# A two-layer graph network on one core: first layer with POOL left to gather, one-input run masks, digits in thirds, re-placed picks and a deferred normalisation

## The chip, the cores and the metric

The kernel runs on 1 core of one Trainium2 chip. The metric is device time in microseconds (us); the median of 3 runs of the kernel before is 3593.15 us (3582.03 to 3596.72).

## The reference

6250 nodes have 128 features, 200,000 edges (sorted by `dst`) have a source, a destination and one of 8 types, and every node has one of 4 types. Two residual layers follow each other:

```
# first layer (x + relu(concat(x, neighbour mean) @ W.T + b), then layer norm)
neigh_sum = segment_sum(x[src], dst)
mean = neigh_sum / max(deg, 1)
neigh_agg = where(deg > 0, mean, x)
x = layernorm(x + relu(concat([x, neigh_agg]) @ W.T + b))
# second layer: typed attention over the edges of each dst
Q, K, V = typed_matmul(x, W_Q | W_K | W_V, node_type)
scores = sum(Q[dst] * typed_matmul(K[src], W_edge, edge_type)) / sqrt(128) * mu[edge_type]
attn = segment_softmax(scores, dst)
x = layernorm(x + segment_sum(V[src] * attn, dst))
```

## The kernel before

Nodes are cut into 49 tiles of 128, edges into columns of 128. The columns are taken in periods of 32; the first layer walks over 49 such periods, one a step (`sweep(l0)`, i = 0 to 48, ND = TILES = 49). Of a period's 32 columns, 14 are fetched by POOL with indirect DMAs ("gathered", two runs of HALF = 7 columns), and 18 (GCOLS) are done on the chip ("dense"), by one-hot masks.

The five instruction streams are written out by hand, and semaphores join them. In each one, the text gives the order in which it executes.

- **POOL**: after setup it issues 98 groups of 7 gathers, group k into buffer k mod 3 (`near`, RUNS = 3), and from the fourth group on it waits before each until TensorE has summed the run that last used the buffer (`runs_ps`). Before the third group it computes `edge_keys()` (src*8 + edge type for every edge, three instructions of 1664 columns), and before the fourth `weights()` (8 small ones on the edge weights).
- **PE** (TensorE), `l0`: 49 matmuls `slot_sum(i, h)`, h = 0 to 48, each of 385 columns, carry the step. Between them stand 18 `pick(i+1, c)` at the h of PICK_AT (they build the next step's one-hot `picked`), the two `run_sum` of 7 matmuls at h = 2 and 23 (RUN_AT), `node_sum` at 6, and the projections of two node tiles: `early` = i-2 (transposes of x and of the mean, the first product) and `late` = i-3 (transpose of the normalised tile at 9, key and value projections at 16 and 18, `low_keys` at 27, `high_keys` at 30).
- **ACT** (ScalarE), `l0`: `take(i+1, c)` copies pick c out of PSUM bank c mod 2, so pick c + 2 waits for it. Between the takes stand `copy_key`, `copy_projected`, `copy_high`, `copy_x`, `copy_mean` and `deviation` (a square root).
- **DVE** (VectorE), `l0`: `hot` builds the masks of 3 picks at a time in a ring of 9 (HOT_RING); `belong(i, h)` builds the 7 masks of a run; `join_parts`, `add_nodes` and `add_runs` add up; `mean`, `relu`, `normalise_x1` belong to the early tile, `by_types` and `copy_low` to the late one. In steps 4 to 12, one `digit_op` (9 in all, 1664 columns each) prepares the second layer's masks.
- **SP** issues the plain DMAs of each tile: the normalised rows and their typed copy to DRAM, the loads of x and of the types two tiles ahead, and the tile's 1 MB of `kv_table` (`store_table`). `store_digits()` is six DMAs, ahead of tile 12.

After the first layer come 98 blocks of the second, each of 16 indirect gathers on POOL (L722) and its attention. The change doesn't touch their code.

Of the kernel before, what the change touches and what calls it, by code (L numbers as in the profile page):

```python
# [6 lines left out]
ALU = mybir.AluOpType  # L7
# [7 lines left out]
P = 128  # L15
# [23 lines left out]
def gnn_kernel(nc, x, src, dst, etype, ntype, w0, b0, wq, wk, wv, we, mu, out):  # L39
# [53 lines left out]
    with ExitStack() as ctx:  # L93
# [47 lines left out]
        iota_g = sb("iota_g", [P, P])  # L141
# [37 lines left out]
        spare_f = spare_n[:, :].bitcast(F32)  # L179
        spare_b = spare_n[:, :].bitcast(BF16)[:, 0:NAT]  # L180
# [28 lines left out]
        near_runs = [near_flat[:, 0:HALF * TW // 2], near_flat[:, HALF * TW // 2:], src_n[:, 0:HALF * TW // 2].bitcast(F32)]  # L209
# [219 lines left out]
        DIGIT_OPS = 9  # L429
        DIGIT_STEP = 4  # L430

# [52 lines left out]
        def _(sp):  # L484
# [85 lines left out]
            for t in range(TILES):  # L570
                if t == 12:
                    sp.wait_ge(digit_vec, DIGIT_OPS)
                    store_digits()
                store(tile(t))
                if t < TILES - 1:
                    store_table(tile(t))
                else:
                    store_last_table(t)
# [73 lines left out]
        def _(pool):  # L652
# [37 lines left out]
            def weights():  # L690
                pool.wait_ge(L["small"], 16)
                pool.wait_ge(L["weights"], 80)
                for e in range(ET):
                    pool.tensor_scalar(we_s[:, e, :], we_s[:, e, :], mu_b[:, e:e + 1], SCALE, ALU.mult, ALU.mult
                                       ).then_inc(weights_ready, 1)

            def edge_keys():
                pool.wait_ge(L["etype"], 48)
                pool.tensor_scalar(spare_n[:, :], src_n[:, :], float(ET), None, ALU.mult).then_inc(pool_step, 1)
                pool.wait_ge(pool_step, 2)  # L700
                pool.tensor_tensor(et_n[:, :], spare_n[:, :], et_n[:, :], ALU.add).then_inc(pool_step, 1)
                pool.wait_ge(pool_step, 3)
                pool.tensor_copy(key_f, et_n[:, :]).then_inc(keys_nat, 1)

            pool.wait_ge(parts_stored, 16 * (TILES // 7))
            pool.wait_ge(tab_copied, TABLES)
            for k in range(2 * ND):
                if k == RUNS - 1:
                    edge_keys()
                    pool.wait_ge(keys_nat, 1)  # L710
                if k == RUNS:
                    weights()
# [29 lines left out]
        def _(pe):  # L742
# [124 lines left out]
            PICK_AT = [-(-c * TILES // GCOLS) for c in range(GCOLS)]  # L867
# [3 lines left out]
            def l0(i, late, early):  # L871
                for h in range(TILES):
# [50 lines left out]
                    if i + 2 < ND and h == TILES - 1:  # L923
                        wait_hot(i + 2, 0)
# [44 lines left out]
            pe.wait_ge(keys_nat, 1)  # L969
# [132 lines left out]
        def _(act):  # L1102
# [64 lines left out]
            def l0(i, late, early):  # L1167
                for c in range(GCOLS):
# [8 lines left out]
                    if late and c == 11:  # L1177
                        copy_high(late)
                    if early and c == 11:
                        copy_x(early)  # L1180
                    if early and c == 13:
                        copy_mean(early)
                    if early and c == 16:
# [79 lines left out]
        def _(dve):  # L1263
# [216 lines left out]
            def digit_op(k):  # L1480

                dve.wait_ge(*((digit_vec, k) if k else (keys_nat, 1)))
                X, Y, Z = (digits[:, i, :] for i in range(3))
                if k == 0:
                    ins = dve.tensor_scalar(spare_n[:, :], dst_n[:, :], 3, 15, ALU.arith_shift_right, ALU.bitwise_and)
                elif k == 1:
                    ins = dve.tensor_scalar(X, spare_n[:, :], -2.0, 16.0, ALU.mult, ALU.add)
                elif k == 2:
                    ins = dve.tensor_scalar(spare_n[:, :], dst_n[:, :], 7, None, ALU.bitwise_and)
# [265 lines left out]
```

## Time and profile before

| | |
|---|---|
| median of the runs | 3593.15 us |
| the profiled execution | 3594.51 us |
| its span, first to last instruction | 3592.7 us |
| mean granted TensorE clock | 0.839 |
| busy PE, DVE, ACT, POOL | 2618.7, 1554.8, 1151.8, 2244.9 us |
| steps of the first layer | 72.6 to 1246.8 us |
| second layer | 1348.0 us to the end |

Busy time counts the engine's own instructions, not its waits; "PEclk" is the share of full speed that TensorE was granted. A row of a timeline has the start, the duration, the engine, line, operation and tiles, and in brackets the idle time before it with what ended it; "issue" and "remote" name no instruction of another engine. TensorE's rows begin when its queue takes an instruction up, and their ends are modelled.

### The profile page before, as it was taken

Reading aid. Unit: us, or ns where it says so; the run is one execution under the profiler, and the core shown is the slowest. Engines: PE = TensorE matmul, PEld = TensorE weight load, DVE = VectorE, ACT = ScalarE, POOL = GpSimd, SP = SyncE. Lnnn points to the kernel's source line nnn. Section 1 sums busy time; section 2 is a strip of 40 time slices with the busy share of each in tenths; the row PEclk is TensorE's granted clock in tenths of the full one; section 3 lists DMA queues with packets and bytes.
Section 4 is the critical chain, followed back from the end, with each engine's and each line's share of the span. In section 5 each row is a group of like instructions: output and inputs, shape, how many; then the busy total and the mean of one; then the engine's idle time right before and its main releaser. Section 6 shows DMA issues by size and latency. Waiting matters only on the chain.

```text
span 3592.7 us, 38408 instructions
## 1 busy us (share of the span) xinstructions
PE 2618.7 (73%) x13802; PEld 1868.6 (52%) x13802; DVE 1554.8 (43%) x4730; ACT 1151.8 (32%) x2057; POOL 2244.9 (62%) x2302
## 2 busy tenths in 40 slices
PE   3587888887878827777777777777777777777777
PEld 1355566555556625555554555555555555555555
DVE  8476677666667613322322233322322333323223
ACT  4344454444444412222222222222222222222222
POOL 7665566566556454666666666666666666666664
PEclk9799999899999968777778887777777877777778
DMA  6244354444444432333333333333333333333332
GB/s 157 62 129 121 111 144 130 120 126 120 119 119 126 118 122 75 100 99 100 100 100 101 103 100 100 99 97 100 100 100 102 102 100 101 100 99 100 101 100 69
DMA packets 256960, 384.03 MB, mean 107 GB/s; under 512 B 100640, under 2 KB 189003, under 8 KB 250625
## 3 DMA queue, kind: packets, MB, share of 16 engines
q0 software_dynamic: 108112, 273.13, 27.6%
q1 hardware_dynamic: 146833, 107.53, 9.7%
q8 instruction: 108, 1.77, 0.2%
q10 hardware_dynamic: 1824, 0.92, 0.1%
q14 instruction: 83, 0.68, 0.1%
HBM read 304.30 MB, written 77.13 MB: 106 GB/s over the span
## 4 chain that ended last, share of the span: by engine, by line
POOL 36%; PE 25%; issue 18%; another core or an unknown queue 13%; DVE 5%; ACT 2%; DMA 0%; ACTq 0%; DVEq 0%; POOLq 0%
POOL ring L722 35%; PE banks L777 9%; PE banks L769 4%; PE banks L803 3%; PE banks L850 1%; PE banks L862 1%; PE banks L992 1%; PE banks L855 1%; PE banks L1005 1%; ACT picks L1138 1%; PE banks L1029 1%; PE banks L865 1%; PE banks L1021 1%; POOL ring L717 1%
## 5 line engine op out<-in xcount | busy, mean ns | idle before, releaser
L722 POOL DMA_INDIRECT ring<-kv_table,src_n x1563 | 1485.4, 950 | 798.3 <-issue 447.6
L1005 PE MATMUL banks<-identf,ring 128*128 128x128 f32 x1568 | 436.9, 373 | 630.4 <-issue 501.1
L717 POOL DMA_INDIRECT ring<-x_part_rows,work x462 | 475.1, 1028 | 307.4 <-PE banks L803 142.8
L1005 PEld LDWEIGHTS banks<-identf,ring 128*128 128x128 f32 x1568 | 250.9, 182 | 791.1 <-issue 585.2
L777 PE MATMUL banks<-sums,picks 128*126 128x385 bf16 x2401 | 608.1, 342 | 33.3 <-ACT picks L1138 15.3
L1138 ACT ACTIVATE picks<-banks 128x343 bf16<-128x343 f32 x882 | 433.3, 512 | 543.7 <-PE banks L769 333.6
L1227 ACT ACTIVATE work<-banks 128x512 f32<-128x512 f32 x392 | 213.5, 598 | 887.6 <-remote 638.9
L1623 DVE SCALAR_TENSOR_TENSOR sums<-sums,corr,banks 128x128 f32<-128x128 f32 x98 | 34.0, 347 | 1029.2 <-remote 1022.6
L1219 ACT ACTIVATE work<-banks,negmax 128x2048 f32<-128x2048 f32 x98 | 192.8, 1968 | 807.9 <-issue 743.7
L777 PEld LDWEIGHTS banks<-sums,picks 128*126 128x126 bf16 x2401 | 331.6, 143 | 149.4 <-issue 54.1
L769 PE MATMUL banks<-sums 128*128 128x343 bf16 x882 | 286.1, 325 | 168.7 <-issue 105.8
L1604 DVE TENSOR_REDUCE largest<-banks 128x1 f32<-128x2048 f32 x98 | 224.5, 2291 | 370.5 <-PE banks L992 273.6
L1029 PE MATMUL banks<-ring,sums 128*128 128x128 f32 x3136 | 372.7, 277 | 5.6 <-issue 4.5
L992 PE MATMUL banks<-work,queries 128*128 128x512 f32 x784 | 372.8, 619 | 0.0
L1029 PEld LDWEIGHTS banks<-ring,sums 128*128 128x128 f32 x3136 | 358.6, 192 | 6.5 <-issue 5.1
L1661 DVE COPY sums<-banks 128x512 f32<-128x512 f32 x392 | 262.5, 689 | 148.6 <-PE banks L1021 101.7
L717 POOL DMA_INDIRECT src_n<-x_part_rows,work x224 | 232.5, 1038 | 136.6 <-issue 60.5
L1021 PE MATMUL banks<-identf,work 128*128 128x128 f32 x1568 | 313.0, 384 | 1.1 <-ACT work L1219 1.1
L1021 PEld LDWEIGHTS banks<-identf,work 128*128 128x128 f32 x1568 | 303.0, 212 | 2.4 <-ACT work L1219 1.3
L1383 DVE TENSOR_SCALAR sums<-iota_k,keys_g 128x344 bf16<-128x344 bf16 x882 | 288.4, 327 | 0.0
L1382 DVE TENSOR_SCALAR sums<-iota_n,keys_g 128x128 bf16<-128x128 bf16 x882 | 238.7, 271 | 114.3 <-PE banks L769 58.9
L992 PEld LDWEIGHTS banks<-work,queries 128*128 128x128 f32 x784 | 144.7, 195 | 189.7 <-issue 189.7
(260 smaller groups left out, 2363.3 us busy)
## 6 DMA issues: line engine op xcount, KB each, us to landing
kv_table<-ring SPq DMA_DIRECT2D x48, 1024.0 KB
ring<-kv_table,src_n POOLq DMA_INDIRECT x1563
sums<-x_typed SPq DMA_DIRECT2D x99, 128.0 KB
x_typed<-work SPq DMA_DIRECT2D x49, 256.0 KB
ring<-x_part_rows,work POOLq DMA_INDIRECT x462
x_part_rows<-sums SPq DMA_DIRECT2D x7, 675.5 KB, 7.1
src_n<-x_part_rows,work POOLq DMA_INDIRECT x224
sums<-x_rows SPq DMA_DIRECT2D x51, 64.0 KB
```

Source lines behind the costliest of these rows:

```text
L717: pool.indirect_dma_start(near[k % RUNS][:, j, :], None, part_dram, bass.IndirectOffsetOnAxis(ap=col_ids[:, first + j:first + j + 1], axis ...
L722: pool.indirect_dma_start(kv_ring[u][:, j, :], None, table, bass.IndirectOffsetOnAxis(ap=of, axis=0)).then_inc(l1_rows[2 * u + j // RUN], 16)
L769: pe.matmul(bank[c % 2][:, 0:KEYS], hot_low[:, c % HOT_RING, :], hot_key[:, c % HOT_RING, 0:KEYS], start=True, stop=True).then_inc(pick_ps, 1)
L777: mm = pe.matmul(bank[2 + i % 2][0:SLOTS, 0:3 * D + 1], picked[:, i % 2, h, 0:SLOTS], x_parts[:, h, 0:3 * D + 1], start=(h == 0), stop=(h ...
L992: mm = pe.matmul(bank[g], queries[:, :], keysT[:, g, :], start=False, stop=True, skip_group_check=True)
L1005: tr = pe.transpose(bank[KEY_BANK[g]][:, j * P:(j + 1) * P], kv_ring[k.u][:, g * 4 + j, 0:D], identf[:, :])
L1021: tr = pe.transpose(bank[PROB_BANK[g]][:, j * P:(j + 1) * P], probT[:, at:at + P], identf[:, :])
L1029: mm = pe.matmul(bank[7][:, 0:D], prob[:, j, :], kv_ring[k.u][:, j, D:2 * D], start=(j == 0), stop=(j == COLS - 1))
L1138: act.activation(picked[:, par, :, c * NW:(c + 1) * NW], bank[c % 2][:, 0:KEYS].rearrange("p (h w) -> p h w", w=NW), ACT.Copy).then_inc(pi ...
L1382: dve.tensor_scalar(hot_low[:, c % HOT_RING, :], iota_n[:, :], keys_g[:, par, 1, c:c + 1], None, ALU.is_equal)
L1383: ins = dve.tensor_scalar(hot_key[:, c % HOT_RING, :], iota_k[:, :], keys_g[:, par, 0, c:c + 1], None, ALU.is_equal)
L1661: dve.tensor_copy(prob[:, g * 4:(g + 1) * 4, :].rearrange("p a b -> p (a b)"), bank[PROB_BANK[g]]).then_inc(prob_copied, 1)
```

## The change

In the first layer alone:

- `edge_keys` and `weights` leave POOL. DVE computes the weights in step 0, and the keys in steps 1 and 2, in four pieces of 416 columns with one fused instruction each. POOL's 98 groups stand back to back. The third run buffer moves from `src_n` to `spare_n`.
- `belong` becomes 7 one-input instructions with a column scalar, on a bf16 `iota_g`, in place of one two-input instruction over 896 elements.
- A `digit_op` covers a third of the columns: 27 of them in steps 4 to 30, after the step's hot masks and no longer at its head. `store_digits` moves from tile 12 to tile 30.
- PICK_AT is no longer even (0, 3, 6, 9, 11, ... 47) but a list. The HOT_AT waits follow from it. The wait for the first masks of the next step moves from h = 48 to h = 2.
- `normalise_x1` moves from the end of DVE's step i to step i+1, behind `join_parts`. ACT's `copy_high`, `copy_x`, `copy_mean` and `deviation` each stand one or two takes later.

```diff
-        near_runs = [near_flat[:, 0:HALF * TW // 2], near_flat[:, HALF * TW // 2:], src_n[:, 0:HALF * TW // 2].bitcast(F32)]
+        near_runs = [near_flat[:, 0:HALF * TW // 2], near_flat[:, HALF * TW // 2:], spare_n[:, 0:HALF * TW // 2].bitcast(F32)]
...
+        DIGIT_COLS = [k * CBLKS // 3 * P for k in range(4)]
+        DIGIT_ALL = 3 * DIGIT_OPS
         DIGIT_STEP = 4
+        KEY_OPS = 4
+        KEY_COLS = [k * NAT // KEY_OPS for k in range(KEY_OPS + 1)]
...
-                if t == 12:
-                    sp.wait_ge(digit_vec, DIGIT_OPS)
+                if t == 30:
+                    sp.wait_ge(digit_vec, DIGIT_ALL)
                     store_digits()
...
             for k in range(2 * ND):
-                if k == RUNS - 1:
-                    edge_keys()
-                    pool.wait_ge(keys_nat, 1)
-                if k == RUNS:
-                    weights()
                 if k >= RUNS:
...
-            PICK_AT = [-(-c * TILES // GCOLS) for c in range(GCOLS)]
+            PICK_AT = [3, 4, 7, 10, 14, 17, 18, 19, 22, 24, 25, 28, 29, 31, 33, 37, 42, 44]
...
-                    if i + 2 < ND and h == TILES - 1:
-                        wait_hot(i + 2, 0)
+                    if 0 < i < ND - 1 and h == 2:
+                        wait_hot(i + 1, 0)
...
-                    if late and c == 11:
+                    if late and c == 12:
                         copy_high(late)
-                    if early and c == 11:
+                    if early and c == 13:
                         copy_x(early)
-                    if early and c == 13:
+                    if early and c == 14:
                         copy_mean(early)
-                    if early and c == 16:
+                    if early and c == GCOLS - 1:
                         deviation(early)
...
-                dve.tensor_tensor(belongs[h], col_keys[:, 1, first:first + HALF].unsqueeze(2).broadcast_to([P, HALF, P]),
-                                  iota_g[:, :].unsqueeze(1).broadcast_to([P, HALF, P]), ALU.is_equal).then_inc(belongs_ready, 1)
+                for j in range(HALF):
+                    ins = dve.tensor_scalar(belongs[h][:, j, :], iota_g[:, :], col_keys[:, 1, first + j:first + j + 1], None,
+                                            ALU.is_equal)
+                ins.then_inc(belongs_ready, 1)
...
+            def weights():
+                dve.wait_ge(L["small"], 16)
+                dve.wait_ge(L["weights"], 80)
+                for e in range(ET):
+                    dve.tensor_scalar(we_s[:, e, :], we_s[:, e, :], mu_b[:, e:e + 1], SCALE, ALU.mult, ALU.mult
+                                      ).then_inc(weights_ready, 1)
+
+            def edge_keys(k):
+                at = slice(KEY_COLS[k], KEY_COLS[k + 1])
                 if k == 0:
...
+                    dve.wait_ge(L["etype"], 48)
+                dve.scalar_tensor_tensor(key_f[:, at], src_n[:, at], float(ET), et_n[:, at], ALU.mult, ALU.add
+                                         ).then_inc(keys_nat, 1)
...
+            def digit_op(n):
+
+                dve.wait_ge(*((digit_vec, n) if n else (keys_nat, KEY_OPS)))
+                part, k = divmod(n, DIGIT_OPS)
+                at = slice(DIGIT_COLS[part], DIGIT_COLS[part + 1])
...
             def l0(i, late, early):
-                if DIGIT_STEP <= i < DIGIT_STEP + DIGIT_OPS:
-                    digit_op(i - DIGIT_STEP)
                 if i > 0:
                     join_parts(i - 1, (i - 1) % 2)
+                if late:
+                    normalise_x1(late)
...
+                if i == 0:
+                    weights()
+                if 1 <= i <= KEY_OPS // 2:
+                    for k in range(2 * i - 2, 2 * i):
+                        edge_keys(k)
+                if DIGIT_STEP <= i < DIGIT_STEP + DIGIT_ALL:
+                    digit_op(i - DIGIT_STEP)
                 if late:
                     copy_low(late)
...
-                if early:
-                    normalise_x1(early)
```

## Rows read from the trace of the kernel before

**Rows 1.** Busy time by stage: us, then PE, PEld, DVE, ACT, POOL, clock, DMA share, GB/s.

```profile
143.50:461.80 318.30, 255.73 (x1437) 176.83 (x1436) 219.78 (x846) 142.62 (x311) 185.48 (x182) 0.94 0.42 116
461.80:1246.80 785.00, 657.21 (x3790) 465.56 (x3790) 546.07 (x2160) 365.46 (x797) 472.84 (x455) 0.94 0.43 124
1348.00:3592.70 2244.70, 1618.79 (x8205) 1169.25 (x8204) 676.06 (x1427) 570.42 (x830) 1439.80 (x1515) 0.79 0.34 98
```

**Rows 2.** The same view, seven steps of 21 us: the first and the sum.

```profile
481.13:502.19 21.06, 18.50 (x113) 13.24 (x113) 16.53 (x67) 10.80 (x25) 14.67 (x15) 1.00 0.48 138
...
sum 147.98, PE 128.65 PEld 92.57 DVE 115.69 ACT 75.87 POOL 102.98; mean PE 18.38 PEld 13.22 DVE 16.53 ACT 10.84 POOL 14.71
```

**Rows 3.** The same view, six steps of 19 us and eight of 30 us: their sums.

```profile
sum 117.10, PE 109.56 PEld 79.65 DVE 96.75 ACT 66.56 POOL 77.28; mean PE 18.26 PEld 13.27 DVE 16.13 ACT 11.09 POOL 12.88
...
sum 236.85, PE 173.06 PEld 117.44 DVE 136.50 ACT 87.56 POOL 129.13; mean PE 21.63 PEld 14.68 DVE 17.06 ACT 10.95 POOL 16.14
```

**Rows 4.** Timeline of POOL behind a step of 30 us, then in one of 21 us.

```profile
1127.33 1.96 POOL L717 DMA_INDIRECT src_n<-x_part_rows,work  x1 [9.78 <-PE banks L803]
...
1148.94 1.68 POOL L717 DMA_INDIRECT ring<-x_part_rows,work  x1 [1.26 <-remote]
1150.93 0.95 POOL L717 DMA_INDIRECT ring<-x_part_rows,work  x1 [0.30 <-issue]
...
1159.62 0.95 POOL L717 DMA_INDIRECT src_n<-x_part_rows,work  x1 [1.43 <-remote]
...
1162.13 1.50 POOL L717 DMA_INDIRECT src_n<-x_part_rows,work  x1 [0.30 <-issue]
...
1170.08 1.68 POOL L717 DMA_INDIRECT ring<-x_part_rows,work  x1 [1.39 <-remote]
```

**Rows 5.** Timeline of DVE in the same step of 21 us: run masks and hot masks.

```profile
1148.71 1.09 DVE L1414 TENSOR_TENSOR ring<-work,iota_g 128x896 bf16<-128x896 f32 x1 [0.58 <-remote]
...
1161.71 1.09 DVE L1414 TENSOR_TENSOR more_belongs<-work,iota_g 128x896 bf16<-128x896 f32 x1
...
1165.69 0.22 DVE L1382 TENSOR_SCALAR sums<-iota_n,keys_g 128x128 bf16<-128x128 bf16 x1
1165.83 0.42 DVE L1383 TENSOR_SCALAR sums<-iota_k,keys_g 128x344 bf16<-128x344 bf16 x1
```

**Rows 6.** Timeline of POOL at the start: the keys, the weights, and groups 3 and 4.

```profile
77.53 4.44 POOL L699 TENSOR_SCALAR spare_n<-src_n 128x1664 int32<-128x1664 int32 x1
...
87.73 1.05 POOL L717 DMA_INDIRECT src_n<-x_part_rows,work  x1 [0.28 <-POOL et_n L703]
...
97.06 3.64 POOL L694 TENSOR_SCALAR ring<-ring,mu_b 128x128 f32<-128x128 f32 x8
100.97 1.01 POOL L717 DMA_INDIRECT ring<-x_part_rows,work  x1 [0.27 <-issue]
```

**Rows 7.** Timeline of PE in step 1 (95.3 to 143.5 us): the two run sums.

```profile
98.71 2.43 PE L803 MATMUL banks<-src_n,ring 128*128 128x385 bf16 x7 [2.87 <-DMA src_n<-x_part_rows,work]
111.33 0.34 PE L803 MATMUL banks<-ring,more_belongs 128*128 128x385 bf16 x1 [4.94 <-DMA ring<-x_part_rows,work]
```

**Rows 8.** Waits of PE from 58.6 to 143.5 us: us in total, times, longest us.

```profile
PE banks L769 <- issue: 18.6, 5, 7.4
```

**Rows 9.** Waits of PE from 461.8 to 1246.8 us, the same columns.

```profile
PE banks L769 <- issue: 68.8, 61, 2.2
...
PE banks L769 <- ACT picks L1138: 26.6, 13, 4.2
```

**Rows 10.** Busy time by stage, steps 4 to 12.

```profile
190.82:409.49 218.67, 177.94 (x1008) 123.20 (x1008) 156.59 (x595) 98.43 (x217) 129.46 (x128) 0.95 0.43 121
```

**Rows 11.** Groups of DVE: busy us, mean ns, then idle time before them.

```profile
L1493 DVE SCALAR_TENSOR_TENSOR digits<-digits 128x1664 bf16<-128x1664 bf16 x1 | 1.9, 1883 | 0.0
...
L1337 DVE SCALAR_TENSOR_TENSOR picks<-picks,ring 128x1664 f32<-128x1664 int32 x1 | 3.5, 3521 | 0.0
...
L1478 DVE COPY ring<-banks 128x512 f32<-128x512 f32 x34 | 23.5, 692 | 83.6 <-remote 60.8 <-PE banks L862 22.0 <-issue 0.8
```

More of the change, by code:

```diff
@@ L140, in gnn_kernel @@
         run_sums = sb("run_sums", [P, D + 1])
-        iota_g = sb("iota_g", [P, P])
+        iota_g = sb("iota_g", [P, P], BF16)
         pick_cols = sb("pick_cols", [P, 3])
@@ L178, in gnn_kernel @@
         key_idx = src_n[:, :].bitcast(U32)
-        spare_f = spare_n[:, :].bitcast(F32)
-        spare_b = spare_n[:, :].bitcast(BF16)[:, 0:NAT]
+        half_b = src_n[:, :].bitcast(BF16)[:, 0:NAT]
         def parts(tile, at, end):
@@ L689, in _ @@
                                         ).then_inc(gen_loaded, 16)
[L690 to L703, printed above, removed]
             pool.wait_ge(parts_stored, 16 * (TILES // 7))
@@ L967, in _ @@
             late_part(tile(TILES - 1))
-            pe.wait_ge(keys_nat, 1)
+            pe.wait_ge(keys_nat, KEY_OPS)
             pe.wait_ge(picked_ready, ND * GCOLS + 2)
@@ L1478, in copy_low @@
                 dve.tensor_copy(kv_of(tile)[:, 0:4, 0:D], by_type(bank[6])).then_inc(kw_low, 1)
-            def digit_op(k):
-                dve.wait_ge(*((digit_vec, k) if k else (keys_nat, 1)))
-                X, Y, Z = (digits[:, i, :] for i in range(3))
-                if k == 0:
-                    ins = dve.tensor_scalar(spare_n[:, :], dst_n[:, :], 3, 15, ALU.arith_shift_right, ALU.bitwise_and)
+            def weights():
[6 more added lines that the diff above has]
+                at = slice(KEY_COLS[k], KEY_COLS[k + 1])
+                if k == 0:
+                    dve.wait_ge(L["etype"], 48)
[5 more added lines that the diff above has]
+                at = slice(DIGIT_COLS[part], DIGIT_COLS[part + 1])
+                X, Y, Z = (digits[:, i, at] for i in range(3))
+                near_dst, spare_d = dst_n[:, at], src_n[:, at]
+                half = half_b[:, at]
+                if k == 0:
+                    ins = dve.tensor_scalar(spare_d, near_dst, 3, 15, ALU.arith_shift_right, ALU.bitwise_and)
                 elif k == 1:
-                    ins = dve.tensor_scalar(X, spare_n[:, :], -2.0, 16.0, ALU.mult, ALU.add)
+                    ins = dve.tensor_scalar(X, spare_d, -2.0, 16.0, ALU.mult, ALU.add)
                 elif k == 2:
-                    ins = dve.tensor_scalar(spare_n[:, :], dst_n[:, :], 7, None, ALU.bitwise_and)
+                    ins = dve.tensor_scalar(spare_d, near_dst, 7, None, ALU.bitwise_and)
                 elif k == 3:
-                    ins = dve.tensor_scalar(Y, spare_n[:, :], -2.0, 8.0, ALU.mult, ALU.add)
+                    ins = dve.tensor_scalar(Y, spare_d, -2.0, 8.0, ALU.mult, ALU.add)
                 elif k == 4:
@@ L1494, in digit_op @@
                 elif k == 5:
-                    ins = dve.scalar_tensor_tensor(spare_b, Y, 0.25, Y, ALU.mult, ALU.mult)
+                    ins = dve.scalar_tensor_tensor(half, Y, 0.25, Y, ALU.mult, ALU.mult)
                 elif k == 7:
-                    ins = dve.tensor_scalar(spare_b, dst_n[:, :], 0.0, FAR_PLACE, ALU.is_lt, ALU.mult)
+                    ins = dve.tensor_scalar(half, near_dst, 0.0, FAR_PLACE, ALU.is_lt, ALU.mult)
                 else:
-                    ins = dve.tensor_tensor(Z, Z, spare_b, ALU.add)
+                    ins = dve.tensor_tensor(Z, Z, half, ALU.add)
                 ins.then_inc(digit_vec, 1)
             def l0(i, late, early):
-                if DIGIT_STEP <= i < DIGIT_STEP + DIGIT_OPS:
-                    digit_op(i - DIGIT_STEP)
                 if i > 0:
                     join_parts(i - 1, (i - 1) % 2)
+                if late:
+                    normalise_x1(late)
                 if i + 1 < ND:
@@ L1558, in _ @@
             join_parts(ND - 1, (ND - 1) % 2)
+            normalise_x1(tile(TILES - 3))
             before, last = tile(TILES - 2), tile(TILES - 1)
```

## The prediction, made before the change was run

> **What bounds the kernel now.** I read the busy time by stage first. The second layer takes 2244.7 of the 3592.7 us, and its code stays; the change works in the first layer, 1103.3 us from step 2 to its end [rows 1]. The later 34 steps take 785.0 us, 23.1 us each, with TensorE busy 657.2 us of them and the granted clock at 0.94 [rows 1]. So TensorE is the fullest engine, but on the mean it stands for 3.8 us of a step, and the question is what for.
>
> The same view step by step shows that a mean step hardly exists. Three kinds stand out among the 33 full later steps: seven of 21.1 us (147.98 / 7) [rows 2], six of 19.5 us (117.10 / 6) and eight of 29.6 us (236.85 / 8) [rows 3]; the other twelve lie between these. TensorE's work is nearly the same in the first two kinds, 18.4 and 18.3 us, so 19.5 us is about what the chain of matmuls needs, and what lies above it is waiting. In the long kind TensorE shows 21.6 us because its clock has dropped, and POOL waits 9.8 us for a run sum behind one [rows 4].
>
> The timeline of POOL says what sets the 21 us kind. A group of 7 gathers starts at 1148.94, the next at 1159.62 and the third at 1170.08: 10.7 and 10.5 us, together one step. Before each start POOL waited only 1.26 to 1.43 us [rows 4]. I read this as a ring of one length: a run sum is seen as done, POOL starts a group, and the next run sum is not seen as done before that group's time has passed. The reader is to see that a group then costs its own length plus some 1.4 us, and that anything that stretches a gather stretches the step. Two gathers of a step are stretched: the usual one is 0.95 us, but those at 1148.94 and 1162.13 take 1.68 and 1.50 [rows 4]. Just then DVE runs its two-input run masks, from 1148.71 and from 1161.71, 1.09 us each [rows 5].
>
> **The change part by part.** The sum is made against the profiled execution, 3594.5 us (span 3592.7, with 1.8 around it); the median of the runs is 1.4 lower.
>
> *Keys and weights leave POOL.* POOL spends from 77.53 to 87.73 us on the keys, 10.2 us, and 3.9 us from 97.06 to 100.97 on the weights [rows 6]. Behind them TensorE waits for the landing of its third and fourth groups, 2.87 and 4.94 us [rows 7]. Both groups now start 10 and 14 us earlier, and both waits go: 8 us. The same stage has 18.6 us of waits ahead of picks, up to 7.4 us each [rows 8]; they fall while POOL gathers without a pause, which it still will. I leave them, and take 0 and 26 us as the ends. On DVE the work comes back as four fused instructions, a quarter of one that takes 3.5 us [rows 11], so 0.9 us each, and eight small weight instructions, by a hot mask of more columns at most 0.4 us each [rows 5], 3 us in step 0. They stand ahead of `copy_low` and `add_runs`. In these steps DVE waits there for a run sum; if that cover is gone, they cost 3 us + 3.5 us.
>
> *Run masks with one input.* They are 14 small instructions a step for two of 1.09 us. The nearest row is the hot mask of the same shape and types: the next instruction starts 0.14 us behind it, and it lasts 0.22 [rows 5]. Seven are 1.0 to 1.5 us, so DVE gains and loses nothing to speak of. POOL gains 0.73 + 0.55 = 1.28 us a step if gathers beside small masks stay at 0.95. They do so now: 18 pairs of hot masks a step run beside the gathers, and the gathers at 1150.93 and 1159.62 take 0.95 [rows 4, 5]. That gain reaches the step only where POOL's ring sets it. Over 45 steps the ends are 0 and 58 us; I take half, 29 us, since the 19.5 us kind and the catching-up steps have other limits.
>
> The Trainium skill (SBUF — State Buffer, Who interferes with whom) says that a vector instruction with two SBUF inputs contends with GpSimd's reads; the rows of the mask agree, 1.68 for 0.95 us. It says too that a one-input copy or tensor_scalar in a two-port mode takes the same port pair for its whole length, which speaks against this change; by that, seven small masks would hold POOL about as long as one large one, and the sum would lose its 29 us. The hot masks' rows don't show it.
>
> *Digits in thirds.* Nine digit instructions of 1.0 to 1.9 us stand at the head of steps 4 to 12 [rows 11], ahead of `join_parts`, on which `node_sum` and the next masks hang. These nine steps take 218.67 us [rows 10], 24.3 each, 1.2 more than the later mean: 11 us in all. I take half, 5 us; the ends are 0 and 11. The 27 thirds cost some 0.4 to 0.6 us each and stand ahead of `copy_low`, where DVE waits 83.6 us over 34 steps, 2.5 a step [rows 11]. Without this cover they would cost up to 14 us. SP's six digit DMAs wait for tile 30 now; the order of the others stays.
>
> *Normalisation a step later.* DVE no longer waits for ACT's square root at its end, and `join_parts` goes ahead of it. The normalised tile is ready about 1 us later, but it is wanted only at h = 9, behind a run sum of 7 matmuls and nine slot sums. SP's store of the tile and the load of x two tiles ahead start later by the same 1 us, and that load is wanted a step later. Nothing, either way; what is late next would be `by_types`, with TensorE's projection at h = 16 behind it.
>
> *Picks and ACT's order.* TensorE's 68.8 us of idle before picks with no named releaser, and the 26.6 us that ACT's take ended [rows 9], are where placement can act. Picks 12 to 17 move up (h = 29 to 44 for 33 to 47), so the ring of masks frees earlier and DVE can run ahead; picks 5, 6 and 7 now stand at 17, 18 and 19, where the two projections lie between them. If those crowd ACT, each waits for a take. From the row I bound both sides at 27 us, and take a third as gain, 9 us.
>
> *Long steps.* Each costs 29.6 - 21.1 = 8.5 us more, eight of them 68 us. They show waits of TensorE and ACT on each other in the second half of the step, and POOL idle behind. The moved picks and the shorter groups both change the phases that lead there; no row says how far. The ends are 68 us gained and 68 lost (twice as many). I take half of them gone, 34 us, since more slack in POOL's ring and earlier masks both pull that way.
>
> Sum: 8 + 29 + 5 + 9 + 34 = 85 us, 3594.5 - 85 = 3509.5, and 1.4 less as a median: **3508 us**. Its own range is 3460 to 3560.
>
> **The rivals.** *All steps in the ring.* Every step takes 21.1 - 1.3 = 19.9 us. The stage from step 2 on is 47 steps in 318.3 + 785.0 us [rows 1], against 47 x 19.9 = 935; with the 8 us of the start the gain is 176 us: 3417. For it speaks that the 19.5 us steps exist [rows 3]; against it, that phases drift again as soon as one wait is missed.
>
> *The small masks hold POOL.* The gathers beside them stay at 1.5 us or more, no 29 us, and the phases stay, no 34: 3594.5 - 22 = 3572. Against it stand the hot masks' rows [rows 4, 5].
>
> *Only the start and the digits count.* Elsewhere TensorE's chain and its hand-overs with ACT set the step, and faster gathers only wait longer: 3594.5 - 8 - 5 = 3581. For it speaks TensorE's 18.4 of 21.1 us.
>
> *More long steps, slower.* Picks at 17, 18, 19 make takes and the key copy queue on ACT, TensorE stands once more in a step, POOL idles 9.8 us as it does behind a long step [rows 4]. At 8.5 us each, five more eat the 42 us of start, masks and digits; eight more give 3594.5 - 42 + 68 = 3620. Against it stands that ACT is busy only 10.8 of 21 us [rows 2].
>
> **How the numbers follow.** Changes under 0.5% (18 us) can't be told from none here: faster is below 3575, slower above 3611. Chances: my forecast 0.45; all in the ring 0.16; masks hold POOL 0.11, of which 0.07 below 3575; start only 0.15; more long steps 0.13. Faster 0.45 + 0.16 + 0.07 = 0.68; same 0.04 + 0.15 = 0.19; slower 0.13. The range takes in the three middle cases and half of the ring case: 3425 to 3605, which leaves out about 0.08 below and 0.12 above.
>
> **What would show it.** Right: step 1 without waits for gathers and well under 48 us; every gather at 0.95 us; seven small masks in 1.0 to 1.5 us; steps 4 to 12 no longer than the later ones; steps of 20 us and at most four of 29; DVE still idle before `copy_low`. Wrong: gathers of 1.5 us beside the masks; TensorE waiting for takes at picks 5 to 7; DVE no longer idle before `copy_low`; as many long steps as before, or more. What would make the number wrong is above all the count of long steps.

## The result and the profile after

The changed kernel takes 3683.89 us (median of 4 runs, 3670.47 to 3685.33) against 3589.63 (4 runs, 3582.03 to 3596.72): ratio 1.0264, interval 1.0224 to 1.0304, 2.6% slower. Predicted were 3508 us, 3425 to 3605.

The profiled execution of after took 3670.5 us. Its page begins (compare the table of the kernel before):

```profile
span 3668.7 us, 39015 instructions
...
PE 2658.7 (72%) x13802; PEld 1881.4 (51%) x13802; DVE 1561.7 (43%) x5348; ACT 1140.3 (31%) x2057; POOL 2206.0 (60%) x2291
```

Busy time of the first layer of after by stage (steps 0 to 2; 3 to 12; 13 to 47). The last line of the first block, and the second block, are the same 29 steps, 18 to 46, in after and in before. Columns: us, PE, PEld, DVE, ACT, POOL, granted clock, DMA share, GB/s.

```profile
78.78:148.78 70.00, 50.07 (x259) 31.98 (x258) 43.36 (x200) 26.33 (x57) 45.85 (x47) 0.89 0.27 67
148.78:407.43 258.65, 203.48 (x1120) 139.45 (x1120) 167.25 (x774) 108.75 (x241) 136.14 (x140) 0.93 0.40 113
407.43:1311.62 904.19, 713.82 (x3921) 485.04 (x3922) 586.01 (x2708) 376.35 (x840) 470.13 (x483) 0.93 0.40 113
...
534.87:1288.72 753.85, 594.44 (x3249) 403.27 (x3249) 486.17 (x2247) 311.79 (x696) 395.34 (x406) 0.93 0.40 114
```

```profile
523.34:1208.83 685.49, 566.94 (x3248) 399.89 (x3248) 475.20 (x1886) 319.64 (x697) 421.39 (x407) 0.93 0.43 123
```

All of the loss is in steps 3 to 47. Steps 0 to 2 take 70.0 us, where before took from 72.64 to 169.54, 96.9 us. But step 48 starts at 1311.62 us for 1231.42, 80.2 us later. The second layer, from its first to its last gather, takes 2281 us for 2283. The three kinds of steps are gone [rows 2, 3]: of the 29 steps none is under 24.2 or over 28.4 us, and the mean is 753.85 / 29 = 26.0 us for 23.6. Of these 2.35 us, (594.44 - 566.94) / 29 = 0.95 are TensorE's busy time and the other 1.4 its idle time.

Two groups of TensorE in the steps of after (485 to 1311 us) show where it stands: slot sums (L760) and picks (L752).

```profile
L760 PE MATMUL banks<-sums,picks 128*126 128x385 bf16 x1556 | 410.0, 340 | 85.2 <-ACT picks L1121 71.9 <-issue 7.3 <-DVE ring L1388 6.0
L752 PE MATMUL banks<-sums 128*128 128x343 bf16 x573 | 185.8, 324 | 89.6 <-issue 51.7 <-ACT picks L1121 37.9
```

Before, from 461.8 to 1246.8 us, the picks had 95.4 us of waits [rows 9], and the slot sums 17.5:

```profile
L777 PE MATMUL banks<-sums,picks 128*126 128x385 bf16 x1666 | 419.7, 341 | 17.5 <-issue 9.4 <-ACT picks L1138 7.9
```

Now the first slot sum of a step waits for the last take of the step before, 71.9 us in all, 2.3 a step. TensorE's timeline in step 31 of after, at h = 13 to 21 and at the start of the next step:

```profile
875.46 0.38 PE L760 MATMUL banks<-sums,picks 128*126 128x385 bf16 x1 [0.93 <-issue]
...
876.25 1.16 PE L833 MATMUL banks<-work,ring 128*128 128x128 f32 x8
...
877.41 0.31 PE L752 MATMUL banks<-sums 128*128 128x343 bf16 x1
...
877.87 1.05 PE L838 MATMUL banks<-ring,work 128*128 128x128 f32 x8
...
880.86 0.32 PE L752 MATMUL banks<-sums 128*128 128x343 bf16 x1 [1.78 <-issue]
...
895.91 0.90 PE L760 MATMUL banks<-sums,picks 128*126 128x385 bf16 x2 [2.35 <-ACT picks L1121]
```

TensorE stands still three times (I call this a stand): 0.93 us at h = 13, where it waits for `add_nodes`; 1.78 at the pick of h = 19, which needs ACT's take of the pick of h = 17; 2.35 at the next step's first slot sum. Behind the two long ones the clock falls (from 881.69 and from 895.69 us; the number behind the five engines is the clock), most of the time to its lower level, 1.2 GHz:

```profile
881.69:885.69 4.00, 3.53 (x12) 1.96 (x13) 1.24 (x6) 2.00 (x4) 0.30 (x1) 0.57 0.00 0
885.69:892.69 7.00, 7.00 (x40) 4.82 (x38) 5.18 (x21) 4.18 (x10) 5.47 (x6) 1.00 0.53 175
895.69:899.19 3.50, 3.28 (x11) 1.73 (x12) 3.33 (x17) 0.46 (x2) 0.00 (x0) 0.54 0.00 0
```

Added up over steps 18 to 46, the stands at the first slot sum are 66.9 us and those at the pick of h = 19 57.8, in all 29 steps; the one at h = 13 is 12.4 us, in 14 of them. The long ones wait for results that come late: in step 31 the first product was recorded to 892.26 us and the pick of h = 44 from 892.42, and ACT and DVE got on with them at 895.36 and 895.31.

```profile
895.31 0.29 DVE L1436 TENSOR_TENSOR ring<-banks,bias_b 128x128 f32<-128x128 f32 x1 [2.52 <-remote]
...
895.36 0.50 ACT L1121 ACTIVATE picks<-banks 128x343 bf16<-128x343 f32 x1 [0.35 <-remote]
```

POOL got what was promised and idles it away. Its gathers of the 29 steps take 974 ns (`ring<-`, x273), but it waits 174.6 us for run sums in that group and 76.9 in the other, 8.7 us a step. And DVE's seven small masks take 1.32 us, as forecast; the next instruction, `add_nodes`, starts 1.13 us behind their start:

```profile
873.87 1.32 DVE L1398 TENSOR_SCALAR ring<-iota_g,work 128x128 bf16<-128x128 bf16 x7
875.00 0.41 DVE L1388 TENSOR_TENSOR ring<-ring,banks 128x258 f32<-128x258 f32 x1
```

### The profile page after: what moved, and what is told of

It reads as the page before. It is cut to its first block, busy times and chain, and to the rows that moved or that the text cites. A ratio compares the mean times of both kernels' runs of the same rounds, so it can differ in the third digit from the quotient of the medians.

```text
span 3668.7 us, 39015 instructions
## 1 busy us (share of the span) xinstructions
PE 2658.7 (72%) x13802; PEld 1881.4 (51%) x13802; DVE 1561.7 (43%) x5348; ACT 1140.3 (31%) x2057; POOL 2206.0 (60%) x2291
## 4 chain that ended last, share of the span: by engine, by line
POOL 38%; PE 23%; issue 17%; another core or an unknown queue 14%; DVE 5%; ACT 3%; DMA 0%; DVEq 0%; ACTq 0%; POOLq 0%
POOL ring L705 38%; PE banks L760 8%; PE banks L752 5%; PE banks L786 4%; ACT picks L1121 2%; PE banks L845 1%; PE banks L833 1%; PE banks L838 1%; PE banks L848 1%; PE banks L775 1%; DVE sums L1366 0%; DVE sums L1365 0%; PE banks L975 0%; ACT work L1202 0%
## 5 line engine op out<-in xcount | busy, mean ns | idle before, releaser
L988 PE MATMUL banks<-identf,ring 128*128 128x128 f32 x1568 | 410.4, 366 | 618.4 <-issue 384.1
L760 PE MATMUL banks<-sums,picks 128*126 128x385 bf16 x2401 | 627.9, 341 | 123.3 <-ACT picks L1121 101.6
L700 POOL DMA_INDIRECT ring<-x_part_rows,work x462 | 449.5, 973 | 398.2 <-PE banks L786 264.0
L760 PEld LDWEIGHTS banks<-sums,picks 128*126 128x126 bf16 x2401 | 339.2, 144 | 257.2 <-ACT picks L1121 117.0
L752 PE MATMUL banks<-sums 128*128 128x343 bf16 x882 | 288.1, 327 | 142.8 <-issue 84.0
L975 PE MATMUL banks<-work,queries 128*128 128x512 f32 x784 | 391.6, 646 | 0.0
L700 POOL DMA_INDIRECT spare_n<-x_part_rows,work x224 | 218.1, 974 | 178.6 <-PE banks L786 115.1
L1004 PE MATMUL banks<-identf,work 128*128 128x128 f32 x1568 | 322.8, 392 | 1.1 <-ACT work L1202 1.1
L1004 PEld LDWEIGHTS banks<-identf,work 128*128 128x128 f32 x1568 | 311.3, 216 | 2.4 <-ACT work L1202 1.3
L1365 DVE TENSOR_SCALAR sums<-iota_n,keys_g 128x128 bf16<-128x128 bf16 x882 | 225.0, 255 | 165.2 <-remote 84.6
```

Source lines behind the costliest of these rows:

```text
L700: pool.indirect_dma_start(near[k % RUNS][:, j, :], None, part_dram, bass.IndirectOffsetOnAxis(ap=col_ids[:, first + j:first + j + 1], axis ...
L752: pe.matmul(bank[c % 2][:, 0:KEYS], hot_low[:, c % HOT_RING, :], hot_key[:, c % HOT_RING, 0:KEYS], start=True, stop=True).then_inc(pick_ps, 1)
L760: mm = pe.matmul(bank[2 + i % 2][0:SLOTS, 0:3 * D + 1], picked[:, i % 2, h, 0:SLOTS], x_parts[:, h, 0:3 * D + 1], start=(h == 0), stop=(h ...
L975: mm = pe.matmul(bank[g], queries[:, :], keysT[:, g, :], start=False, stop=True, skip_group_check=True)
L988: tr = pe.transpose(bank[KEY_BANK[g]][:, j * P:(j + 1) * P], kv_ring[k.u][:, g * 4 + j, 0:D], identf[:, :])
L1004: tr = pe.transpose(bank[PROB_BANK[g]][:, j * P:(j + 1) * P], probT[:, at:at + P], identf[:, :])
```

## The experiments

**Two kinds of chips.** The first four sittings of experiments fell on four chips where the kernel before takes 3013 to 3017 us instead of 3590, with the same instructions; the fifth fell on one where it takes 3643. So a time is compared with that of the kernel before in its own sitting alone. I call the four quick, and the other two the first kind. Step means below are over steps 18 to 46 of a trace.

| kernel | kind of chip | median us | before | ratio (interval) | step us |
|---|---|---|---|---|---|
| before_again (1 run) | quick | 3016.2 | 3016.9 | | 18.36 |
| after_again | quick | 3029.4 | 3016.9 | 1.0043 (1.0026 to 1.0059) | 18.88 |
| picks_back | quick | 3083.9 | 3014.6 | 1.0228 (1.0211 to 1.0245) | 20.09 |
| act_back | quick | 3056.2 | 3014.6 | 1.0142 (1.0125 to 1.0159) | 19.54 |
| norm_back | quick | 3031.7 | 3014.6 | 1.0055 (1.0038 to 1.0071) | 18.91 |
| picks_alone | quick | 3061.9 | 3014.6 | 1.0155 (1.0138 to 1.0172) | 19.40 |
| three_back | quick | 3028.2 | 3016.9 | 1.0038 (1.0024 to 1.0053) | 18.92 |
| masks_alone | quick | 3036.0 | 3016.9 | 1.0064 (1.0047 to 1.0081) | 18.93 |
| relief | quick | 3006.3 | 3013.1 | 0.9976 (0.9966 to 0.9985) | 18.39 |
| relief_touch | quick | 2997.8 | 3013.1 | 0.9950 (0.9933 to 0.9966) | 18.39 |
| before_four | quick | 3149.3 | 3012.7 | 1.0454 (1.0433 to 1.0475) | 21.15 |
| after_four | quick | 3156.1 | 3012.7 | 1.0476 (1.0455 to 1.0497) | 21.56 |
| before_product | first | 3716.2 | 3643.3 | 1.0184 (1.0130 to 1.0237) | 24.95 |
| after_product | first | 3907.5 | 3643.3 | 1.0708 (1.0652 to 1.0764) | 30.24 |
| masks_back | first | 3577.8 | 3643.3 | 0.9810 (0.9737 to 0.9883) | 23.08 |

**The three reorderings** (picks_back, act_back, norm_back, picks_alone).

```diff
picks_back:
-            PICK_AT = [3, 4, 7, 10, 14, 17, 18, 19, 22, 24, 25, 28, 29, 31, 33, 37, 42, 44]
+            PICK_AT = [-(-c * TILES // GCOLS) for c in range(GCOLS)]
-                    if 0 < i < ND - 1 and h == 2:
-                        wait_hot(i + 1, 0)
+                    if i + 2 < ND and h == TILES - 1:
+                        wait_hot(i + 2, 0)
act_back: copy_high, copy_x, copy_mean, deviation at c == 12, 13, 14, GCOLS - 1 -> 11, 11, 13, 16
norm_back: normalise_x1(late) behind join_parts -> normalise_x1(early) at the end of DVE's step
picks_alone: the kernel before with the lines that picks_back takes out
```

picks_back: 

> The changed kernel with the old even places of the picks (0, 3, 6, 9, ...) and the wait for the first hot masks back at the last slot sum; all else as changed. Theory P, the places of the picks cost the time (TensorE waits 2 to 4 us a step at the pick of h = 18, between the two projections): the time falls under that of the kernel before, to some 3550 us. Theory A, the order of ACT's copies does (the square root stands at the last take and that take is what the next step's first slot sum waits for): 3660 to 3690. Theory N, the deferred normalisation: 3660 to 3690.

act_back: 

> The changed kernel with ACT's copies back at takes 11, 11, 13 and 16. Theory P: 3670 to 3690. Theory A: under 3600 us, and the wait of TensorE's first slot sum for the last take (66.7 us over 32 steps) goes. Theory N: 3670 to 3690.

norm_back: 

> The changed kernel with the normalisation of a tile back at the end of its own step on DVE. Theory P: 3670 to 3700 (DVE waits a little for the square root again). Theory A: about 3684, or more, as DVE now waits for a square root that ACT does last. Theory N: under 3600 us.

picks_alone: 

> The kernel before with nothing but the new places of the picks and the wait for the first hot masks at h = 2. Theory P: about 3684 us or more, since nothing of the rest's gain is in it: 3680 to 3720. Theories A and N: 3580 to 3600, as before.

(The stand that the expectation puts at h = 18 is the one at h = 19.) None of the three theories held on these chips, in an unexpected way: undoing the picks alone or ACT's order alone makes the changed kernel slower, by 1.2 and 0.66 us a step, and the new picks alone make the kernel before slower by 1.04. The two belong together. A second run of picks_back on another quick chip gave the same, 1.0227 (1.0209 to 1.0244): 

> The changed kernel with the old places of the picks alone, once more. On a chip whose TensorE results come on time: 2.3% over the kernel before, as measured. On a chip like that of the first comparison, if the new places of the picks cost the time there: within 1% of before.

Undoing the normalisation changes nothing there (18.91 for 18.88 us). None of these runs fell on a chip of the first kind.

**The unchanged pair, all three undone, the masks alone.** before_again is the kernel before; after_again the changed one; three_back undoes picks, ACT's order and normalisation at once; masks_alone is the kernel before with this:

```diff
-        iota_g = sb("iota_g", [P, P])
+        iota_g = sb("iota_g", [P, P], BF16)
...
-                dve.tensor_tensor(belongs[h], col_keys[...].unsqueeze(2)..., iota_g..., ALU.is_equal)
+                for j in range(HALF):
+                    ins = dve.tensor_scalar(belongs[h][:, j, :], iota_g[:, :], col_keys[:, 1, first + j:first + j + 1], None, ALU.is_equal)
```

before_again: 

> The kernel before, unchanged, for a trace from a chip of this pair of sittings: if it is the chip of the first four kernels, 3014 us with a first layer of regular steps of 18.5 to 19 us and no long ones; if it is that of the first comparison, 3590 us with the mixture of 19.5, 21.1 and 29.6 us.

after_again: 

> The changed kernel, unchanged. Theory P (places of the picks cost 2 us a step, whatever the clock) and theory N (the deferred normalisation costs 1 us a step): steps of 20 to 21 us where the clock stands at full, 1.5 to 3% over the kernel before. Rival, the loss belongs to the throttled clock alone: within 0.5% of the kernel before on a chip whose clock is full.

three_back: 

> The changed kernel with the places of the picks, ACT's order and the normalisation all as before; it keeps POOL's relief, the one-input masks and the thirds of the digits. If these three parts give what the prediction said (8 + 29 + 5 us): 1.2% under the kernel before. If gathers of 0.95 us reach no step where the clock is full: only the start, 0.3 to 0.6% under. If one of them costs: over it.

masks_alone: 

> The kernel before with nothing but the seven one-input masks. If a step hangs on POOL's ring: 0.8% under the kernel before (0.6 us for each of 48 steps). If it hangs on TensorE's and DVE's hand-overs: within 0.3%.

On a quick chip each step is like the last (18.34 to 18.37 us before), and one part accounts for the whole of the step's loss: the masks alone cost 0.57 us a step, as much as the whole change (0.52), and the three reorderings together nothing (18.92 with them undone; the reorderings without the masks were not run on a quick chip). Three undone once more, on another quick chip, gave 1.0037 (1.0024 to 1.0050): 

> The changed kernel with the places of the picks, ACT's order and the normalisation as before, once more. On a chip whose TensorE results come on time: 0.4% over the kernel before, as measured. On a chip like that of the first comparison: if the places of the picks or ACT's order cost the 2.6% there, within 0.5% of before or under it; if the masks and digits do, 2% over.

Steps 18 to 46 of before_again and of masks_alone, busy time:

```profile
429.15:961.63 532.48, 520.46 (x3248) 388.21 (x3248) 460.07 (x1886) 321.06 (x697) 408.60 (x406) 1.00 0.56 159
```

```profile
430.75:979.73 548.98, 527.49 (x3249) 385.85 (x3249) 484.74 (x2234) 321.07 (x697) 393.14 (x407) 1.00 0.54 154
```

TensorE is busy 520.46 of 532.48 us: here it is the bound, and POOL's 15.5 us less of busy time (408.60 to 393.14) reach nobody. DVE has 24.67 us more, 0.85 a step. The waits of these steps, before_again first:

```profile
PEld banks L777 <- ACT picks L1138: 22.8, 29, 0.8
...
ACT rstd L1151 <- DVE aggr L1455: 8.7, 29, 0.3
```

```profile
PEld banks L777 <- ACT picks L1138: 33.4, 30, 1.3
...
ACT rstd L1151 <- DVE aggr L1457: 18.2, 29, 0.9
...
PEld banks L850 <- DVE work L1473: 8.5, 29, 0.3
...
PEld banks L777 <- DVE ring L1405: 6.2, 29, 0.2
```

Each step now waits for DVE three times: 0.2 us for `add_nodes` (L1405), 0.3 for `by_types` (L1473), and once more, through ACT's square root and the take behind it, at the first slot sum, where the loads' wait goes from 0.8 to 1.1 us. In the changed kernel TensorE's only stand is at the first of these, 0.66 us at h = 13 of each step:

```profile
414.45 0.38 PE L760 MATMUL banks<-sums,picks 128*126 128x385 bf16 x1 [0.66 <-DVE ring L1388]
```

The masks of masks_alone take 1.31 us for 1.08 to 1.09; counted from start to next start, DVE spends 0.27 us a step more on them and 0.23 on the hot masks of 344 columns (mean 335 ns for 310). That adds up to 0.5 us, but it doesn't show that these are what the step pays for: DVE still waits 48.9 us in these steps ahead of `copy_low`, and in after_again the run masks take 0.28 us more and the hot masks nothing, for the same loss. Shown is that the masks cost it, and where TensorE then waits.

**What a relieved POOL gives, and 9 ns.** relief is the changed kernel without masks and reorderings: keys and weights on DVE, digits in thirds. It differs from three_again, of the same sitting, by the masks alone, and takes 3006.3 us for 3023.5: once more some 0.5 us a step. relief_touch has in addition, between group 3 and group 4 of the gathers (their waits on each other left out here):

```diff
+                pool.memset(touched[:, :], 0.0)
+                pool.tensor_scalar(whole[:, 0:2], whole[:, 2:4], float(ET), None, ALU.mult)
+                pool.tensor_tensor(whole[:, 4:6], whole[:, 0:2], whole[:, 2:4], ALU.add)
+                pool.tensor_copy(touched[:, 6:8], whole[:, 4:6])
+                pool.tensor_scalar(touched[:, 0:2], touched[:, 6:8], touched[:, 2:3], SCALE, ALU.mult, ALU.mult)
```

relief: 

> The kernel before with the keys and weights on DVE and the digits in thirds, nothing else of the change. On a chip whose TensorE results come on time: steps of 18.4 us from step 3 on, 18 us gained in steps 0 to 2 and some 11 us in steps 4 to 12, and 13 us lost in the second layer, where a gather takes 957 ns for 948 once the keys and weights are off POOL: 3000 us against 3016. If the gathers' 9 ns come from the masks' or another part: 2987. On a chip like that of the first comparison the same parts give 3570 against 3590.

relief_touch: 

> The same with five instructions of 2 to 8 columns on POOL between the first three groups of gathers and the rest (fill, multiply, add, cast, multiply by a column). If it is the running of such instructions that makes each later gather 9 ns shorter: 948 ns again and 13 us less, 2987 us. If it is something else that moved with the keys (a tile's place, a semaphore): 957 ns and the time of the kernel beside it.

touch_again, the same kernel on another quick chip: 

> The kernel before with keys, weights and digits moved and five small instructions on POOL, once more: 0.5% under the kernel before on a chip whose TensorE results come on time. On a chip like that of the first comparison: the start's 18 us and little else, 0.5% under as well.

Against before_again, relief is 15.8 us ahead at step 3 (125.21 for 141.04) and 25.8 at step 13 (311.52 for 337.36), so the start gives 16 us and the digits 10. Then it loses 15.3 us in the second layer (1973.8 us from first to last gather for 1958.5). Its gathers there, of before_again, relief and relief_touch:

```profile
L722 POOL DMA_INDIRECT ring<-kv_table,src_n x1563 | 1482.2, 948 | 476.5 <-issue 476.5
```

```profile
L705 POOL DMA_INDIRECT ring<-kv_table,src_n x1563 | 1497.4, 958 | 476.7 <-issue 476.7
```

```profile
L721 POOL DMA_INDIRECT ring<-kv_table,src_n x1563 | 1483.8, 949 | 476.2 <-issue 476.2
```

All 1563 gathers are 9 to 10 ns longer once POOL no longer runs the keys and weights, and five instructions of at most 8 columns bring that back. touch_again took 2996.97 us, ratio 0.9950 (0.9933 to 0.9966), like relief_touch. relief and relief_touch came out 6 and 11 us above what I had expected (3000 and 2987), but on a quick chip both beat both kernels, relief_touch the kernel before by 0.5%. Neither was run on a chip of the first kind. There the 9 ns cost nothing that can be seen: 2281 us for 2283 in the first pair, and in the fifth sitting 2300 us with gathers of 949 ns (before_product) and with 960 (masks_back).

**Late results put in by hand.** In the first pair of traces TensorE's results come after their recorded ends. ACT's timeline shows it best: picks 5 and 6 (recorded at 877.41 and 877.72 in step 31 of after) and ACT's takes of them:

```profile
880.20 0.61 ACT L1121 ACTIVATE picks<-banks 128x343 bf16<-128x343 f32 x1 [3.68 <-remote]
...
881.60 0.83 ACT L1121 ACTIVATE picks<-banks 128x343 bf16<-128x343 f32 x2 [0.69 <-PE banks L752]
```

and the same two takes in after_again, whose pick 5 starts at 661.95:

```profile
662.30 0.61 ACT L1121 ACTIVATE picks<-banks 128x343 bf16<-128x343 f32 x1 [1.23 <-PE banks L752]
...
662.91 0.50 ACT L1121 ACTIVATE picks<-banks 128x343 bf16<-128x343 f32 x1
```

The take comes 0.35 us behind the pick's start on the quick chip and 2.79 on the other. So I made such delays: in before_four and after_four `for t in list(range(NT)) * 4` in `project_values`, in before_product and after_product 24 extra matmuls of 128 columns ahead of the two of `first_product`. The added results are overwritten by the real ones. The two additions are not of one size, though I took them to be. A matmul on f32 has two records of 0.112 us: at the value projection 8 records a step become 32, 2.7 us more, but at the first product 48 come on top, 5.4 us.

```profile
611.27 5.52 PE L830 MATMUL banks<-ring 128*128 128x128 f32 x48
```

before_four: 

> The kernel before with the eight matmuls of the value projection done four times over, so that their result and all behind it come 24 x 0.112 = 2.7 us later in each of 48 steps. If TensorE is what a step hangs on: 2.7 us a step, 130 us in all. If part of it is hidden by waits: less.

after_four: 

> The changed kernel with the same. If its picks at 17, 18 and 19 and its last take are what makes it suffer more from late results: at least 1 us a step more than the kernel before with the same, 180 us or more in all. If it is no more exposed: the same 130 us.

before_product: 

> The kernel before with 24 more matmuls of 128 columns ahead of the first product at h = 42, 2.7 us a step. TensorE is what a step hangs on, so some 2.7 us a step, 130 us in all.

after_product: 

> The changed kernel with the same. If its last takes, 16 and 17 with the square root behind them, are what makes it suffer from a late result there: at least 1 us a step more than the kernel before with the same, 180 us over its own time. If not: the same 130 us over its own time.

At the value projection the changed kernel is no more exposed: both steps grow alike, 18.36 to 21.15 and 18.88 to 21.56 us. At the first product, on the chip of the first kind, it is: the kernel before pays 73 us for some 260 us of added work (5.4 us for each of 49 tiles; I had expected 130 for 130), and has the clock at full throughout steps 18 to 46 (first window below), while the changed kernel's steps go from 26.0 (in the first comparison) to 30.2 us, with the clock at 0.93 (second). It takes 191 us more than the kernel before with the same addition, in the same sitting.

```profile
569.59:1293.26 723.67, 684.06 (x4640) 540.87 (x4640) 474.86 (x1886) 319.34 (x697) 421.65 (x406) 1.00 0.41 117
```

```profile
605.51:1482.49 876.98, 746.43 (x4641) 562.59 (x4641) 488.48 (x2248) 311.61 (x696) 392.44 (x406) 0.93 0.35 98
```

Not where I expected, though: the stand is no longer at the first slot sum but at the pick of h = 19 (103.3 us in 27 of the 29 steps):

```profile
677.08 0.32 PE L752 MATMUL banks<-sums 128*128 128x343 bf16 x1 [3.81 <-ACT picks L1123]
```

**The masks on a chip of the first kind.** masks_back is the changed kernel with the two-input masks (the diff of masks_alone the other way round), in the same sitting as the two above. 

> The changed kernel with the two-input masks of 896 columns back. If the seven small masks are the whole of the 0.5 us a step: steps of 18.4 us and 24 us less than the changed kernel, 3003 us for a kernel before of 3015. If the deferred normalisation ahead of the masks holds TensorE at h = 13 by itself: steps of 18.7 us, 3018. On a chip like that of the first comparison: 1% less than the changed kernel if the masks cost there what they cost here, no change if the late results hide them.

It is 1.9% faster than the kernel before of its sitting (interval 1.2 to 2.6%), where the changed kernel was 2.6% slower in the first. Steps 18 to 46:

```profile
514.46:1183.84 669.38, 555.60 (x3249) 382.40 (x3249) 477.86 (x1893) 310.89 (x696) 415.43 (x406) 0.98 0.46 128
```

A step takes 23.1 us for 26.0 with the small masks; 1.34 us of the difference is TensorE's busy time (clock 0.98 for 0.93) and 1.57 its idle time. The gathers are long again (1027 ns for 974), which costs nothing that can be seen. So the masks are what turns a gain of some 2% into a loss. TensorE's waits ahead of slot sums in steps 18 to 46, of before, of after (three lines) and of masks_back:

```profile
PE banks L777 <- ACT picks L1138: 6.4, 8, 1.2
...
PE banks L760 <- ACT picks L1121: 69.4, 30, 2.7
PE banks L760 <- issue: 6.4, 7, 0.9
PE banks L760 <- DVE ring L1388: 6.0, 7, 0.9
...
PE banks L760 <- ACT picks L1121: 21.5, 17, 2.7
PE banks L760 <- issue: 11.5, 19, 0.7
PE banks L760 <- DVE ring L1388: 2.5, 4, 0.8
```

What the masks changed on this kind is not the wait for `add_nodes` behind them: the stand at h = 13 comes to 12.4 us in after and 13.0 in masks_back. It is the two waits for late results: at the first slot sum 66.9 us against 20.6, at the pick of h = 19 57.8 against 11.1. By the semaphore events of the traces, the first product's result comes 2.7 us behind its recorded end in after (mean over the first layer), 1.4 in masks_back and 0.9 in before; that of the value projection 3.5, 3.0 and 1.55 us. So with the small masks TensorE's results came later still; why, no run shows.

The caution: the changed kernel was not timed in that sitting, and the conditions were not the same (the kernel before 3590 and 3643 us; the second layer, from first to last gather, 2281 and 2300). That the changed kernel is slower in the fifth sitting too is seen only with the added matmuls, 3907.5 us for 3716.2.

## Why the prediction was wrong, step by step

*Run masks with one input, -29 us: this step failed.* Its durations were right: gathers of 0.97 us beside the small masks, seven in 1.32 us. Wrong was that POOL's ring sets part of the steps, so that shorter gathers shorten them: they got to 974 ns, and POOL waited the longer. Wrong too was "so DVE gains and loses nothing to speak of". What the runs showed: on quick chips +0.57 us a step, some 26 us over 45 steps, with TensorE standing for `add_nodes`, `by_types` and the first slot sum; on the first kind +2.9 us a step, 130 us over 45, with TensorE standing at the pick of h = 19 and at the first slot sum, for results that come late. I had priced the masks on POOL and on DVE's sum, and not on TensorE, which is what a step hangs on. With +130 for -29 the sum would be 3667 us, against 3684 measured. masks_back is 65 us under its kernel before, where the other terms sum to 56; that is no proof of them one by one, since no kernel before without additions was traced in that sitting and the largest of them, the long steps, didn't come about as forecast.

*Long steps, -34.* This failed as well. The 29.6 us kind did go, and the 19.5 us kind with it, the wrong way: every step from 18 to 46 takes 24 to 28 us. I took 19.5 us for what TensorE's chain needs and the long steps for accidents on top of it. The quick chips show 18.36 us for every step of the same program: on the first kind all steps carry some 5 us of late results and stands, and the kinds are how these fell.

*Keys and weights, -8.* Right in kind, too small: -15.8 on the quick chip, and 20.8 us at step 3 in the first pair, inside the ends of 0 and 26. What I didn't see is that POOL's gathers get 9 ns longer, 13 us in the second layer of after_again and 15 in that of relief.

*Digits in thirds, -5.* -10.0 on the quick chip, near the upper end of 0 to 11. On the first kind it can't be told apart: steps 3 to 12 of after take 25.9 us each, no longer than its later ones, as forecast.

*Normalisation, 0.* Held on the quick chips (18.91 for 18.88 us); not tried on the first kind.

*Picks and ACT's order, -9, ends ±27.* Together 0 on the quick chips. There, one without the other costs 31 to 57 us over 47 steps; that they can only be moved together was not in the prediction. On the first kind they were never undone.

*The rivals.* The masks do not hold POOL. On the first kind no kernel had a mean step near 19.9 us, and the start and digits alone were not all that counted. "More long steps, slower" had the right side and one right place, takes late behind the picks at 17, 18 and 19: TensorE waits for one at h = 19 in each of the 29 steps. Whether the new places alone would have cost anything there is open. before_four and after_four speak against it, but on a quick chip; masks_back speaks against it too, since with the same places it is faster than the kernel before. What the prediction held against this rival, ACT busy only half of the step [rows 2], was no argument: ACT waited for TensorE. No rival had the masks cost anything beyond the gain that they were to bring.

*What stays open.* Why small masks cost 0.6 us a step where TensorE's results come on time and 2.9 where they don't. The clock is part of it (0.98 without the small masks, 0.93 with them, 1.34 of the 2.9 us as longer matmuls). But the kernel before has 0.93 in the same steps too, so by itself it doesn't set the two apart. What makes TensorE's results late on some chips, and later with the small masks, is open: in step 31 the granted clock reads 1.00 while it happens.

## What to carry to other kernels

When an instruction is split to spare another engine, price it on the engine that bounds the step, which may wait for an instruction behind it: on the quick chips, run masks that take 0.13 us longer cost every step 0.57 us. An engine's time saved counts only where that engine is on the path, and the same profile may give other paths on other chips: repeat the kernel before in each sitting, and doubt a term that needs a chain to stay as one execution shows it. Places in one engine's hand-written order and in its partner's are one edit; on the quick chips, half of it cost 3 to 6% of a step.

## What the chip showed that I had not expected

- The same kernel took 3013 to 3017 us on four chips and 3590 to 3643 on one or two others. On the quick ones TensorE's results come 0.01 us behind the recorded ends. In the first comparison those of the value projection came 1.55 us behind on the mean of 45 steps in the kernel before, whose mean step is 23.6 us for 18.36, and 3.5 us in the changed kernel, in step 31 at a granted clock of 1.00.
- Added TensorE work of 5.4 us a step at the first product cost the kernel before 73 us on the chip of the first kind (some 260 us were added), and 2.7 us a step at the value projection cost 137 on a quick one (130 were added). The trace of the former shows no time at the lower clock in steps 18 to 46, where that of the kernel before in the first comparison shows 92 us.
- A gather takes 9 ns less, 948 to 949 ns for 957 to 958, once POOL has run a few tensor instructions, down to 2 columns; it holds for all 1563 of the second layer. Which of the five does it was not tried.
- Seven one-input masks of 128 columns leave the gathers at 0.97 us on the mean, where the two-input mask of 896 columns makes those beside it 1.5 to 1.7 [rows 4].
